# Film block of a transformer kernel: 64 head blocks of 100 rows become one stream of 50 tiles of 128 rows, and the 32 kept values are found by a threshold

## The reference, cut to what matters

```python
Q = (x_text @ Wq).reshape(Bb, Tt, H, DH)          # H = 4, DH = 32
K = (x_vision @ Wk).reshape(Bb, Gg, H, DH)        # Gg = 1444
scores = jnp.einsum('bthd,bghd->bhtg', Q, K) / np.sqrt(DH).astype(np.float32)
scores = jnp.where(vision_mask[:, None, None, :], scores, -jnp.inf)
topv, topi = jax.lax.top_k(scores, K_TOP)         # K_TOP = 32
probs = jax.nn.softmax(topv, axis=-1)
attn = jnp.zeros_like(scores).at[bi, hi, ti, topi].set(probs)
attn_mean = attn.mean(axis=1)                     # over the 4 heads
c_t = jnp.einsum('btg,bgd->btd', attn_mean, x_vision @ Wv) * text_mask[..., None]
```

## Time and profile before

| | |
|---|---|
| time, median of 3 runs | 5149.49 us (5117.75 to 5162.92) |
| profiled execution: span from first to last instruction | 5139.5 us |
| Film block, first MAX8 to end of the last copy of ct | 3804.76 to 4654.54 us |
| PE, DVE, ACT, POOL busy in the whole span | 4115.3, 2994.6, 2115.7, 1733.6 us |

### The profile page before, as it was taken

How to read it: one execution, slowest core, us unless ns; L and a number is a source line. 1 busy time by engine, 2 the same in 40 slices (tenths; PEclk the granted TensorE clock), 3 DMA queues, 4 the chain that set the end, 5 groups by cost and what they waited for, 6 DMA issues and landing times. The chain is left out here.

```text
span 5139.5 us, 86857 instructions
## 1 busy us (share of the span) xinstructions
PE 4115.3 (80%) x26550; PEld 2846.4 (55%) x26550; DVE 2994.6 (58%) x4577; ACT 2115.7 (41%) x3227; POOL 1733.6 (34%) x1171
## 2 busy tenths in 40 slices
PE   8899999999979988778789999994763434336699
PEld 4588888888867746534445555552432222223377
DVE  4344445444523444446545676656459999996433
ACT  3255555555522232124324555542235555551122
POOL 2266666666524232004310000000225555541033
PEclk8799999999969988799867999996876666667699
DMA  2000000000002203220022222210010101000011
GB/s 85 1 10 19 10 19 19 19 10 19 10 1 62 59 1 91 48 61 2 1 56 47 65 62 62 62 33 1 1 24 18 26 17 26 17 19 1 0 61 48
DMA packets 124607, 152.80 MB, mean 30 GB/s; under 512 B 86912, under 2 KB 110224, under 8 KB 124080
## 3 DMA queue, kind: packets, MB, share of 16 engines
q1 hardware_dynamic: 124208, 147.72, 11.5%
HBM read 109.43 MB, written 2.66 MB: 22 GB/s over the span
## 5 line engine op out<-in xcount | busy, mean ns | idle before, releaser
L989 POOL TENSOR_TENSOR pexp_lo<-arena,pexp_hi 128x800 fp32r<-128x800 f32 x384 | 635.7, 1655 | 443.2 <-POOLq L988 442.5
L2173 DVE TENSOR_REDUCE arena<-ps 100x1 f32<-100x482 f32 (+1 forms) x768 | 489.9, 657 | 266.8 <-DVEq L2160 256.5
L2053 DVE TENSOR_REDUCE arena<-ps 128x1 f32<-128x482 f32 (+3 forms) x624 | 392.9, 656 | 365.6 <-DVEq L2031 354.8
L1330 ACT ACTIVATE arena<-ps 128x800 f32<-128x800 f32 x384 | 322.3, 839 | 500.3 <-ACTq L1328 497.8
L2471 DVE MATCH_REPLACE8 arena<-arena 100x1444 f32<-100x1444 f32 x256 | 420.8, 1656 | 0.0
L1420 ACT ACTIVATE arena<-ps 128x800 f32<-128x800 f32 x384 | 315.5, 837 | 249.8 <-ACTq L1419 243.6
L3202 PE MATMUL ps<-kst,qs 96*100 96x482 f32 (+1 forms) x768 | 376.2, 492 | 43.0 <-PEq L3156 39.4
L935 POOL TENSOR_TENSOR max_diag<-w_const,arena 100x800 fp32r<-100x800 f32 x160 | 246.8, 1543 | 436.5 <-POOLq L933 436.5
L3331 PE MATMUL ps<-w_const,w_cross 100*128 100x100 f32 x192 | 43.2, 380 | 374.1 <-PEq L3328 374.1
L1331 ACT ACTIVATE pexp_hi<-ps 128x800 fp32r<-128x800 f32 x384 | 319.5, 832 | 0.0
L2573 DVE TENSOR_TENSOR arena<-ps,arena 128x400 f32<-128x400 f32 x256 | 147.1, 575 | 280.2 <-DVEq L2572 280.2
(11 more groups left out here) (393 smaller groups left out, 9621.0 us busy)
## 6 DMA issues: line engine op xcount, KB each, us to landing
ctxT<-in_ctxT SPq DMA_DIRECT2D x56, 541.5 KB
kst<-mid SPq DMA_DIRECT2D x128, 180.5 KB, 3.1
ctxk<-in_ctx SPq DMA_DIRECT2D x40, 528.0 KB
chunk<-in_ff_chunks SPq DMA_DIRECT2D x77, 193.0 KB, 2.4
arena<-gate_dram SPq DMA_DIRECT2D x64, 200.0 KB, 3.8
kst<-xn SPq DMA_DIRECT2D x64, 180.5 KB, 2.9
arena<-gate_dram SPq DMA_DIRECT2D x64, 100.0 KB, 2.6
arena<-in_ctxT SPq DMA_DIRECT2D x8, 541.5 KB
```

The lines of the kernel that those rows point to most:

```text
L989: own(nc.gpsimd.tensor_tensor(pexp_lo[p % 3][:, :, :], pexp[p % 3], pexp_hi[p % 3][:, :, :], ALU.subtract))
L1330: nc.scalar.activation(pexp[p % 3], of, ACT.Exp, scale=scale).then_inc(s.pexp_ready, 1)
L2053: peak = nc.vector.tensor_reduce(mparts[0:at.stop - at.start, m, c:c + 1], bank(k, z - a, at.stop - at.start), AX.X, ALU.max)
L2173: peak = nc.vector.tensor_reduce(mparts2[:, h, c:c + 1], bank(k, z - a, S), AX.X, ALU.max)
```

## The change

All rows of all heads and batches are put one after another, 6400 rows, and cut into 50 tiles of 128. 14 tiles hold rows of two batches; such a tile gets two score products that add up in the same banks, each with the query columns of the other batch set to zero (`qv` has 112 zero columns on both sides). Every engine's list is unrolled over slots k = -6 to 53 (`FILM_SLOTS`).

DVE finds the 32 greatest values of a tile with four MAX8 and three MATCH_REPLACE8; the last striking out goes. The 32nd value is the threshold. ACT takes the sign of (threshold - score) over all 1444 columns with its sum, and over the 32 values; from the two sums POOL counts the ties, and the places that are left are shared among the tied ones: weight = relu(share - sign), cut to at most 1 by POOL, then multiplied with exp(score - greatest). The subtraction, the scaling of 1444 columns and the additions of heads go. Head mean, division and turning become products on PE: kept (128 rows x 1444) against `token`, a 128 x 100 selection matrix with 1/4 of the inverse sum where a row belongs to a token, 12 products for each tile and batch, added up over the tiles in three banks (3 to 5). There is one set of score banks (0 to 2) instead of two. SP issues a batch's columns apart from its tokens, in another order, and the text mask after the first four loads. ACT's 21 diagonal matrices (`lag_diag`) are made in slots 10 to 30.

```diff
@@ SP
+            columns(0)
+            columns(1)
+            tokens(0)
+            tokens(1)
             sp.dma_start(text_mask.bitcast(U8), ...)
-            load(0, 0)
-            load(1, 1)
-            with sp.Fori(0, B // 2 - 1) as i:
-                load(2 * i + 2, 0)
-                load(2 * i + 3, 1)
+            columns(2)
+            for b in range(2, B):
+                if b + 1 < B:
+                    columns(b + 1)
+                tokens(b)
@@ POOL
+            def ties(i):
+                pool.wait_ge(s.totals, 1)
...
+                own(nc.gpsimd.tensor_scalar(stat_of(i, SPARE), stat_of(i, OVER), 2.0, float(K), ALU.mult, ALU.add))
+                own(nc.gpsimd.tensor_tensor(stat_of(i, TIES), stat_of(i, SPARE), stat_of(i, SIDE), ALU.subtract))
+                pool.sem_inc(s.ties_ready, 1)
+            def keep(i):
+                pool.wait_ge(s.expd_ready, 1)
...
+                own(nc.gpsimd.tensor_scalar(taken[i % 2], taken[i % 2], 1.0, None, ALU.min))
+                own(nc.gpsimd.tensor_tensor(kept[i % 3], kept[i % 3], taken[i % 2], ALU.mult))
+                pool.sem_inc(s.taken_free, 1)
+                pool.sem_inc(s.kept_ready, 1)
+            for k in FILM_SLOTS:
+                for b in range(B):
+                    if first_tile(b) == k + 5:
+                        mask(b % 2)
+                if 0 <= k - 1 < STREAM:
+                    ties(k - 1)
+                if 0 <= k - 2 < STREAM:
+                    keep(k - 2)
+                if 0 <= k - 1 < STREAM:
+                    shares(k - 1)
@@ ACT
+            def counts(i):
+                act.wait_ge(s.taken_ready, 1)
...
+                own(nc.scalar.activation(low[:, i % 3:i % 3 + 1], tops[:, i % 3, 0:1], ACT.Copy, scale=-1.0))
+                nc.scalar.activation(top_exp, tops[:, i % 3, :], ACT.Exp, bias=..., accum_out=stat_of(i, DEN))
+                own(nc.scalar.activation(top_side, tops[:, i % 3, :], ACT.Sign, ..., accum_out=stat_of(i, OVER)))
+                if i >= 2:
+                    act.wait_ge(s.taken_free, 1)
+                    act.sem_inc(s.taken_free, -1)
+                own(nc.scalar.activation(taken[i % 2], scores_sb[i % 4], ACT.Sign, ..., accum_out=stat_of(i, SIDE)))
+                act.sem_inc(s.totals, 1)
+            def tokens(i):
+                act.wait_ge(s.scale_ready, 1)
...
+                    nc.scalar.activation(token[i % 3][:, n, :], W("const", "token_of_row")[:, off:off + S], ACT.Copy, scale=by)
+                own(nc.scalar.activation(taken[i % 2], taken[i % 2], ACT.Relu, bias=stat_of(i, SHARE), scale=-1.0))
+                act.sem_inc(s.expd_ready, 1)
+            for k in FILM_SLOTS:
+                if 0 <= k - 1 < STREAM:
+                    counts(k - 1)
+                for b in ending(k - 3):
+                    mean()
+                if 0 <= k - 2 < STREAM:
+                    tokens(k - 2)
+                if 0 <= k - 1 < STREAM:
+                    exponents(k - 1)
+                if 0 <= k + 3 < STREAM:
+                    scores(k + 3)
+                for b in starting(k + 6):
+                    queries(b)
+                for b in ending(k - 3):
+                    values()
+                for b in ending(k - 4):
+                    features(b)
...
-        act.sem_inc(s.row_scores_free, 2)
+        act.sem_inc(s.row_scores_free, 1)
@@ DVE
+            def reciprocals(i):
+                dve.wait_ge(s.ties_ready, 1)
+                dve.sem_inc(s.ties_ready, -1)
+                nc.vector.reciprocal(stat_of(i, DEN, 2), stat_of(i, DEN, 2)).then_inc(s.shares_asked, 1)
+            for k in range(-1, STREAM + 1):
+                early, late = k + 1 < STREAM, 0 <= k < STREAM
+                if early:
+                    greatest(k + 1, 0)
+                if late:
+                    greatest(k, 2)
...
+                if early:
+                    without(k + 1, 1)
+                if late:
+                    finished(k % 2)
+                    dve.sem_inc(s.taken_ready, 1)
+                if 0 <= k - 1:
+                    reciprocals(k - 1)
@@ PE
+            def mean(i, b):
+                first = b in starting(i)
                 for t in range(KT):
                     r = key_rows_of(t)
+                    ins = mm(bank(3 + t // 4, S, r, t % 4 * S), kept[i % 3][:, 128 * t:128 * t + r], token[i % 3][:, batches_of(i).index(b), :],
+                             start=first and t % 4 == 0, stop=b in ending(i), skip_group_check=True)
+                return ins
...
+            for k in FILM_SLOTS:
+                if 0 <= k + 4 < STREAM:
+                    scores(k + 4)
+                for b in starting(k + 6):
+                    queries(b)
+                for b in ending(k - 4):
+                    features()
+                if 0 <= k - 3 < STREAM:
+                    upper(k - 3)
+                for b in ending(k - 3):
+                    sums(b)
+                if 0 <= k - 2 < STREAM:
+                    lower(k - 2)
```

More of the change, by code:

```diff
@@ L1449, in own, with queries @@
                 act.sem_inc(s.act_done, -1)
-            def queries():
+            def queries(b):
                 act.wait_ge(s.proj_full, 1)
                 act.sem_inc(s.proj_full, -1)
-                own(nc.scalar.activation(qv[0:C, :, :], bank(6, TH * S, C).rearrange("p (h t) -> p h t", t=S), ACT.Copy))
+                own(nc.scalar.activation(qv[b % 2][0:C, QAT:QAT + TH * S], bank(6, TH * S, C), ACT.Copy))
                 act.sem_inc(s.proj_free, 1)
                 act.sem_inc(s.qv_ready, 1)
[L1458 to L1469, removed]
@@ new lines, in mean @@
+            def mean():
+                act.wait_ge(s.turn_full, 1)
+                act.sem_inc(s.turn_full, -1)
+                for n in range(KT // 4):
+                    full = 4 if n < KT // 4 - 1 else 3
+                    ins = nc.scalar.activation(meanT[:, 4 * n:4 * n + full, :], bs(bank(3 + n, full * S)), ACT.Copy)
+                own(nc.scalar.activation(meanT[0:KTAIL, KT - 1, :], bank(3 + KT // 4 - 1, S, KTAIL, 3 * S), ACT.Copy))
+                act.sem_inc(s.mean_free, 1)
+                act.sem_inc(s.mean_ready, 1)
@@ L1539, in film_block, with features @@
-            queries()
-            scores(0)
-            batch(0, 0, first=True)
-            with act.Fori(0, B // 2 - 1) as i:
-                batch(2 * i + 1, 1)
-                batch(2 * i + 2, 0)
-            batch(B - 1, 1, last=True)
-            for j in range(PE_LAGS):
-                ins = nc.scalar.activation(lag_diag[:, j, :], W("const", "ident"), ACT.Copy, scale=kernel_l[:, j:j + 1])
-            own(ins)
+            def features(b):
+                act.wait_ge(s.u_full, 1)
+                act.sem_inc(s.u_full, -1)
+                own(nc.scalar.activation(ct[:, b:b + 1, :], bs(bank(7, S)), ACT.Copy))
+                act.sem_inc(s.turn_free, 1)
@@ L3343, in mean, with features @@
+            def features():
                 pe.wait_ge(s.uv_ready, 1)
                 pe.sem_inc(s.uv_ready, -1)
-                pe.wait_ge(s.proj_free, 1)
-                pe.sem_inc(s.proj_free, -1)
-                mm(bank(6, S), W("tk", "wv"), uv, start=True, stop=True).then_inc(s.proj_full, 1)
-            def batch(b, par, first=False):
-                if not first:
-                    mean(1 - par)
-                queries(b + 1)
-                for h in range(TH):
-                    scores(h, 1 - par)
@@ L3356, in film_block @@
-            queries(0)
-            for h in range(TH):
-                scores(h, 0)
-            batch(0, 0, first=True)
-            with pe.Fori(0, B // 2 - 1) as i:
-                batch(2 * i + 1, 1)
-                batch(2 * i + 2, 0)
-            mean(0)
-            mean(1)
+                mm(bank(7, S), W("tk", "wv"), uv, start=True, stop=True).then_inc(s.u_full, 1)
+            pe.sem_inc(s.turn_free, 1)
+            for k in FILM_SLOTS:
[11 more added lines that the diff above has]
+                    lower(k - 2)
```

339 lines of the change are left out of this document (160 added, 179 removed).

## The result

The changed kernel takes 5229.5 us (median of 4 runs, 5197.9 to 5272.0), the kernel before 5149.2 (4 runs): ratio of the runs 1.0174, 95% interval 1.013 to 1.0219 (the two medians alone give 1.0156). The forecast was 5185 with a range of 5090 to 5270: the time is inside it, the sign was held open, and the point is 44 us too low.

A forecast was written before the change was run, and what follows sets the result against it. DVE set the film stage's end (849.8 us); after the change ACT's in-order waits would: 53.4 us per batch times 16 = 854, plus 32 for mask and loads = 886, rounded to +35 on 5149.5: 5185 us, range 5090 to 5270.

The forecast's parts named there:

- mask and loads: In eight batches POOL's mask waits for loads queued behind ACT's uv copy: 4 us each, 32 us.
- ACT's own work with handoffs: ACT's copies, Exp, Sign, Relu, evictions and diagonal copies over the film stage: 509 us, 31.8 per batch.
- sums and features: ACT waits in order for PE's uv, query and ct products: 9.9 and 5.4 us per batch.
- mean: ACT waits for a batch's last selection product on PE, behind POOL's keep and a score product: 4.2 us per batch.
- Sign: ACT's full-width Sign waits for POOL's minimum and multiply to free a buffer: 1.9 us in 1.1 slots, 2.1 per batch.
- Rival 1: DVE goes on setting the pace: stage 599 us, kernel 4898 us; chance 4%.
- rival 2: PE keeps 2.4 GHz, so ACT's waits for it are shorter: kernel 5077 us; chance 10%.
- rival 3: PE hardly leaves 1.2 GHz, so ACT's waits for it are longer: kernel 5320 us; chance 8%.
- The minimum, 2.54 us: POOL's one-operand minimum over 128x1444, priced at half of the 5.07 us two-operation uint8 row.
- rival 4: POOL's minimum costs 5.07 us like the uint8 row, about 20 us per us: kernel 5235 us; chance 15%.
- the fill: ACT idles about 11 us in the first tile, set against the last batches without a score product ahead.
- rival 5: Sign or Relu on ACT need another table, two loads a tile, 128 us: kernel 5313 us; chance 4%.

The follow-up runs named there:

- e4: Changed kernel with PE doing sums, queries and features products ahead of the score product: stage 777.0 us against 925.1, kernel 5074.6 us, ratio to before 0.9846.
- e5: Changed kernel with POOL's minimum and multiply done as one pass on DVE: stage 860.9 us against 925.1, kernel 5158.2 us, ratio to before 1.0042.
- e1: Changed kernel with SyncE issuing columns of batch b+2 ahead of tokens of batch b: stage 893.3 us against 925.1, kernel 5212.6 us.
- e8: Changed kernel with DVE doing each tile's third MAX8 four times, 150 more passes: stage 942.3 us against 925.1, kernel 5234.7 us.
- e7: Changed kernel with 20 filler passes on PE before score products that follow a pause: stage 875.0 us against 925.1; no kernel time given.
- e9: Changed kernel with a second operation, multiplication by 1, in POOL's minimum: stage 938.1 us against 925.1, kernel 5221.7 us (one run).
- e2: Changed kernel without POOL's minimum, so its output differs: stage 867.3 us against 925.1, kernel 5144.0 us, ratio to before 0.9997.
- e3: Changed kernel with PE doing only the sums ahead of the score product: stage 816.7 us against 925.1, kernel 5123.7 us.

## Why the prediction was right in kind and 44 us low

The forecast's chain: DVE is relieved, ACT's in-order waits take over, mask and loads add 32 us. Its terms against the trace, for the whole stage. From the waits of after I take what is left of the same waits where an edit had removed them, as that is handoff and belongs to ACT's own work (uv, queries and ct by e4's rows, the Sign's by the 9.6 us that e5 leaves):

| term | forecast | measured |
|---|---|---|
| ACT's own work with handoffs | 509 | 506 |
| sums and features (queries, uv, ct) | 244 | 230 |
| mean | 67 | 79 |
| Sign 34, mask and loads 32 | 66 | 90 |
| evictions and tokens | 0 | 20 |
| stage | 886 | 925 |

The 230 are the 253 of the three waits less e4's 23. Of evictions and tokens (21.7 + 21.3) their usual handoff goes off, 0.20 and 0.27 each. The mean's wait, which no edit removed, is taken whole; own work is what remains. e1 takes the 90 apart: without the masks' waits the Sign has 61.8 - 9.6 = 52, so that it stands at 52 against 34 and mask and loads at 38 against 32.

- *DVE 563 us, 257 removed*: right, 566 busy. That this is worth nothing where ACT paces: right, shown by e8. Rival 1 (4898) had called for DVE to stay full; it idles 323 us.
- *ACT's waits for PE, 9.9 + 5.4 a batch*: right in place, and in the sum nearly right in size (230 against 244). Batches 0 to 3 and 8 to 11 have about 6.02 + 4.65 and 5.89, less some 0.4 each. The forecast took all batches alike, and they are not: in batches 4 to 7 ACT waits 10.6 to 14.1 for uv and 5.7 to 6.9 for the queries in two different slots, and 0.33 for ct, 73.7 us in the four against 61 of the forecast. The clock was read rightly: the score product after a pause goes at 1.2 GHz, what follows at 2.4, and e7 shows that it goes with the pause. Rivals 2 and 3 had one clock throughout; the trace has both.
- *Mask and loads, 32 us in b = 2 to 5 and 10 to 13, whose copies hold up the masks of batches 4 to 7 and 12 to 15*: right, the very eight, and 31.8 us by e1.
- *The minimum, 2.54 us*: **this is the term that was mis-sized**. It takes 3.86, past the 3.4 from which rival 4 was to decide. It does so in all 50 tiles (3.85 to 3.86), in the last one with DVE idle beside it. "Half of the two-operation row" took the price for proportional to the operations; e9 shows 3.86 for the first and 1.22 for the second. What each us is worth was also off, in the other direction: 20 in the forecast, 14 by e2 and 11 by e9, since the Sign's wait and the mean's are not both on the path in every batch. So the 1.32 us cost 14 to 19 of the 39 missing in the stage, and the 18 by which the Sign alone was too low fit that. The Sign does not wait in every slot, which would have spoken against the forecast, but in 28 of 50 tiles for more than a handoff. Rival 4's figure, 5235, close as it lies to 5229.5, comes from a price and a slope that were both too high.
- The Trainium skill, GPSIMD Engine Reference, section Engine selection, has one-input operations on GpSimd at roughly line rate. The trace agrees for the cast of the earlier trace rows (1.39 us, 0.96 ns an element), which the forecast took only as a lower bound. It does not agree for the minimum: 3.86 us over 1444 elements is 2.67 ns each, more than the 3.24 us of the two-input multiply beside it.
- *Costed at nothing*: evictions and tokens, 20 us, and the last tile. Some 12 of the 20 are two evictions in the first tiles (waits of 4.74 and 7.16 us); with 16.0 us of three waits for queries there, the fill is 28 us, not 11. The forecast set it against the last batches, which have no score product ahead, and in batches 13 to 15 the waits for uv and ct come to 14.7 us where three batches of the forecast have 46: the two nearly cancel. What was missed is the last tile, where nothing is left that ACT could do beside POOL and PE: it waits 6.33 us before its last token copy (0.27 to 0.62 in the other tiles) and 13.50 before the last turned mean. That is 15 of the 39 us, and a sum of sixteen equal batches has no place for it. The tail that was to "stay near 29" is 58, from the end of the last MAX8 (4726.2 + 1.67) to the end of the stage.
- *The class*: "within 1%" had 0.50 and slower 0.37; it is slower, by 1.6 to 1.7%. The forecast put a part of the slower share on the prices of Sign and handoffs; own work was right, and it came from the minimum (18), the last tile (15) and the masks (6); the rest, fill, mean and the waits for PE, adds up to about nothing. Of the 44 us, 39 are the stage's; the other 5 are less than the chance spread of the stages ahead of it.
- *Table loads* (rival 5): the stage has one, 1.28 us ahead of its first Exp; Sign and Relu bring none.
- *The mean, 4.2 a batch*: 65.9 us in fifteen batches, 4.4 each; 9 of the 12 us too many are the one wait in the last batch. It does not follow the minimum: without it the wait is 108 (e2), with a longer one 62 (e9), so a part of what ACT does not wait before the Sign it waits here.
- Two prices of the working do not follow from its rows. The queries' 0.9 us at 1.2 GHz is the 0.85 of the earlier trace rows, which ran at a granted clock of 1.00, the 2.4 GHz level; with 24 passes taking 4.5 at 1.2 GHz, 8 take 1.5. The 2.0 us of the mean at 2.4 GHz are not worked out; 1.62 score products of 2.5 would be 4.05. The first makes rival 3 some 10 us too low and the forecast about 1, the second would make rival 2 some 33 too low.

Left open: how far the stage varies between runs of one kernel, and with it the last few us of each term.

## What to carry to other kernels

When a change relieves the busiest engine, cost the in-order lists of the others next: here the order in which PE issued the same products was worth twice the loss. Put short products that another engine waits for ahead of a long one that still has to wait for its input; in e3 they also filled the pause that had put the long one at the lower clock. Count the last tile by itself, since the waits that other work covers in the stream are open there. A price for one operation out of a row with two takes a second row; half is a guess.

## What the hardware showed that was not expected

- On POOL a one-input minimum over 128x1444 float32 takes 3.86 us, with a second operation 5.07, the two-input multiply 3.24; on DVE minimum and multiply in one instruction take 1.66.
- 20 filler passes ahead of a score product shorten it from 4.95 to 2.66 us: work that no one needs paid for itself, and with 26 such groups the stage came out 50 us shorter. The sums, moved to the same place, do the same (2.66 in e3).
- The stages ahead of the film stage, unchanged, differ by up to 83 us from run to run (start of the first MAX8 3778.2 to 3860.8), with a granted clock over the first 3778 us of 0.91 in the earliest, 0.88 in the latest, and 0.89 in the two next to it (3847 and 3850).
